# First layer of a graph network: the row gathers in fours with a wait for their landing, in place of waits for VectorE's marks

## Chip, cores and metric

One core of a Trainium2 chip runs one launch of the kernel. The metric is the time of the launch on the device in microseconds (us), lower is better. TensorE, VectorE, ScalarE, GpSimd (POOL in the profile) and SyncE (SP) each have an instruction stream of their own and meet through semaphores.

## The reference

Four graph layers run one after the other on 3,125 nodes of 64 features and 100,000 edges sorted by destination. Only the first concerns this change:

```python
Qh = (x @ Wq.T + bq).reshape(n, H, D)          # H = 4 heads of D = 16
Kh = (x @ Wk.T + bk).reshape(n, H, D)
Vh = (x @ Wv.T + bv).reshape(n, H, D)
Ee = (edge_attr @ We.T + be).reshape(-1, H, D)
score = (Kh[src] * Qh[dst] * (1.0 / np.sqrt(D)) * Ee).sum(-1)
score = jnp.exp(jnp.clip(score, -5.0, 5.0))
msg = Vh[src] * score[..., None]
wV = jax.ops.segment_sum(msg, dst, num_segments=n)
x = _layernorm(x + wV.reshape(n, H * D))
```

The other three layers (a LightGCN, a graph attention, and an attention on edge features) follow, each with a layernorm.

## The kernel before

**Stages.** After a start in which the K and V rows of all nodes are computed and stored in HBM as the table `kv_tab` (one row of 128 floats a node), the first layer goes over the edges in G = 98 groups of 1,024 edges, 8 edges (C = 8) on each of 128 partitions. In the same loop the kernel counts edges between pairs of node tiles (`key_hot`, `lo_hot`, `count`) for the later layers. Then come the layernorm, preparations, and layers two to four; none of those is touched.

**A group on each engine.** SP loads the group's 1,024 source numbers (`idx`) and its edge attributes (`ea`, 256 KB). POOL issues 8 indirect DMAs (line 634), one for each column c, each of which gathers 128 rows of `kv_tab` into `kv[:, s, c, :]`; `kv` and `ea` have RS = 4 slots s, so that a group's rows can be gathered while up to three older groups are unread. VectorE multiplies the K rows with the edge products (line 704) and the queries (line 712), sums over heads (714), clips (716), adds four blocks of counts (698), builds the next group's one-hot matrix (676) and, with ScalarE's exponential, the message (725), then the next group's eight `key_hot` (683), and last adds TensorE's 64-node window of sums to `acc` (736). TensorE counts (837), transposes (795, 803), sums the messages (852) and makes the next group's products (812 to 820).

**What sets the order around the change.** VectorE's line 736 waits for `sum_ok`, which TensorE raises with its last matmul of line 852, and itself raises `slot_free`, on which SP waits before it loads `idx` and `ea` for the group four further on. POOL waits for `idx_in[s]`, so it can never gather into a slot whose reader isn't done. Beside that it waits for `half_done`, a count that starts at 3 and that VectorE raises twice a group, with line 712 and after line 725. By these numbers the second four gathers of a group wait for line 712 of the group before, and the next group's first four follow them at once. VectorE waits for `kv_in[s]` to reach 128 (8 gathers by 16) before line 704. `pass_on` adds 1 to a counter nobody waits for; it turns a wait against a register into one instruction of the engine's queue.

In the rows `shared` is the buffer in which `kv` and `ea` lie, so "shared<-kv_tab,idx" is one gather.

Of the kernel before, what the change touches and what calls it, by code (L numbers as in the profile page):

```python
# [8 lines left out]
ALU, ACT, AX = mybir.AluOpType, mybir.ActivationFunctionType, mybir.AxisListType  # L9
# [7 lines left out]
C = 8  # L17
ST = P * C
G = -(-E // ST)
# [46 lines left out]
def build(nc, x, src, dst, edge_attr_2, edge_attr_64, Wq, bq, Wk, bk, We, be, Wv, bv,  # L66
          attn_w, W_fc, W_attn, W_edge, W_e2n, W_m1, W_m2, out):
    ctx = ExitStack()
    with ctx:
# [9 lines left out]
        def short_sem(name):  # L79


            return nc.alloc_semaphore(name=name)
# [92 lines left out]
        bank = [ctx.enter_context(nc.psum_tensor(f"bank{i}", [P, 512], fp32)) for i in range(8)]  # L175
# [351 lines left out]
        def pass_on(eng):  # L527

            eng.sem_inc(passed, 1)
# [27 lines left out]
        prod = sb("prod", [P, C * D])  # L557
# [21 lines left out]
        def uses(s):  # L579
# [8 lines left out]
        cleared, q_in = short_sem("a_cleared"), short_sem("a_queries")  # L588
        key_ok, lo_ok, count_ok, bank_free = short_sem("a_key"), short_sem("a_lo"), short_sem("a_count"), short_sem("a_count_added")
        count_clear = short_sem("a_count_cleared")  # L590

        half_done = short_sem("a_half_done")
        loop_sems = [begun, slot_free, *idx_in, *ea_in, hot_ok, ea_t, ea_ts, hot_t, hot_ts, ee_ok, qd_ok, sc_ok, ex_ok, msg_ok, sum_ok,
                     cleared, q_in, key_ok, lo_ok, count_ok, bank_free, count_clear, half_done]
        nc.clear_and_free_semaphores(early_sems)
        with nc.Block() as block:
            @block.sync
# [21 lines left out]
            @block.gpsimd  # L619
            def _(pool):  # L620
                nj = sweeps(pool, 1)
                with pool.Fori(0, nj) as j:
                    def gather(g, s, m):

                        pool.wait_ge(half_done, (j * G + g) * 2 + 1)
                        pass_on(pool)
                        pool.wait_ge(idx_in[s], (j * uses(s) + m) * 16)
                        pass_on(pool)
                        for c in range(C):
                            if c == C // 2:  # L630

                                pool.wait_ge(half_done, (j * G + g) * 2 + 2)
                                pass_on(pool)
                            nc.gpsimd.indirect_dma_start(  # L634
                                kv[:, s, c, :], None, kv_tab, bass.IndirectOffsetOnAxis(ap=idx[:, s, c:c + 1], axis=0)
                            ).then_inc(kv_in[s], 16)

                    each(pool, gather)
                    forget_rows(pool, kv_in, slot_free, cleared, (j + 1) * G + RS)

            @block.vector
            def _(dve):
                nj = sweeps(dve, 1)

                dve.sem_inc(slot_free, RS)
                dve.sem_inc(half_done, 3)
                dve.sem_inc(cleared, 1)
                nc.vector.memset(count_i[:, 0:NT * 2 * D], 0)
                nc.vector.memset(msg[:, :, D:D + 1], 1.0)
                nc.vector.memset(qwin[:, :, :, :], 0.0)  # L650
                nc.vector.memset(ones_b[:, :], 1.0)
                rest = be_row[:, :]
                for k in range(BF):
                    nc.vector.tensor_copy(be_part[:, k, :], rest)
                    dve.drain()
                    if k + 1 < BF:
                        nc.vector.tensor_tensor(be_rest[:, k, :], rest, be_part[:, k, :], ALU.subtract)
                        dve.drain()
                        rest = be_rest[:, k, :]
                nc.vector.tensor_scalar(be_rest[:, 0, :], be_part[:, 0, :], ident[0:BF, 0:1], None, ALU.mult)  # L660
                dve.drain()
                for k in range(1, BF):
                    nc.vector.scalar_tensor_tensor(be_rest[:, k % 2, :], be_part[:, k, :], ident[0:BF, k:k + 1], be_rest[:, (k - 1) % 2, :], ALU.mult, ALU.add)
                    dve.drain()
                nc.vector.tensor_copy(be_parts[:, :, :], bc(be_rest[:, (BF - 1) % 2, :], 1, C))
                reset_windows(dve, True)
                dve.sem_inc(bank_free, 2)
                dve.wait_ge(count_clear, 1)
                with dve.Fori(0, nj) as j:
                    dve.wait_ge(cleared, j + 1)  # L670
                    pass_on(dve)
                    start_sweep(dve, begun, True)

                    def node_hots(g, s, m):

                        nc.vector.tensor_tensor(hots[:, s % 2, :, :], bc(dst_rel[:, bass.ds(g, 1), :].rearrange("p g c -> p (g c)"), 2, W),
                                                bc(iota[:, 0:W], 1, C), ALU.is_equal).then_inc(hot_ok, 1)

                    def key_hots(g, s, m):

                        keys = tile_key[:, bass.ds(g, 1), :].rearrange("p g c -> p (g c)")
                        for c in range(C):
                            last = nc.vector.tensor_scalar(key_hot[:, c, :], iota_key[:, :], keys[:, c:c + 1], None, ALU.is_equal)  # L683
                        last.then_inc(key_ok, 1)

                    def front(g, s, m):
                        node_hots(g, s, m)
                        key_hots(g, s, m)

                    def step(g, s, m, after):  # L690

                        n = j * G + g + 1

                        def add_counts(q):

                            at = count[:, :, bass.ds(group_at[q], WC)]
                            dve.wait_ge(count_ok, j * (G * GG) + g * GG + q + 1)
                            nc.vector.tensor_tensor(at, at, bank[6 + q % 2][:, 0:KC].rearrange("p (h w) -> p h w", w=WC),  # L698
                                                    ALU.add).then_inc(bank_free, 1)

                        kvs = kv[:, s, :, :]
                        dve.wait_ge(kv_in[s], m * (16 * C))
                        dve.wait_ge(ee_ok, n)
                        nc.vector.tensor_tensor(prod[:, :].rearrange("p (c f) -> p c f", c=C),
                                                bank[3][:, :].rearrange("p (c f) -> p c f", c=C), kvs[:, :, 0:D], ALU.mult)
                        b, *group_at = nc.values_load_multi_w_load_instructions(
                            base_i[0:1, bass.ds(g, 1), 0:1 + GG].rearrange("a g k -> a (g k)"), engines=[mybir.EngineType.DVE],
                            min_val=0, max_val=NP,
                            skip_runtime_bounds_check_because="start_sweep keeps them within 0 and NP")[1]
                        dve.drain()  # L710
                        dve.wait_ge(qd_ok, n)
                        nc.vector.tensor_tensor(prod[:, :], prod[:, :], bank[4][:, :], ALU.mult).then_inc(half_done, 1)  # L712
                        dve.drain()
                        nc.vector.tensor_reduce(score[:, :], prod[:, :].rearrange("p (a d) -> p a d", d=DH), AX.X, ALU.add)
                        dve.drain()
                        nc.vector.tensor_scalar(score[:, :], score[:, :], -5.0, 5.0, ALU.max, ALU.min).then_inc(sc_ok, 1)  # L716

                        add_counts(0)
                        if after:

                            node_hots(*after)
                        dve.drain()
                        add_counts(1)
                        dve.wait_ge(ex_ok, n)
                        nc.vector.tensor_tensor(msg[:, :, 0:D].rearrange("p c (h d) -> p c h d", h=H),  # L725
                                                kvs[:, :, D:2 * D].rearrange("p c (h d) -> p c h d", h=H),
                                                bc(expo[:, :].rearrange("p (c h) -> p c h", h=H), 3, DH), ALU.mult).then_inc(msg_ok, 1)
                        dve.sem_inc(half_done, 1)
                        for q in range(2, GG):
                            dve.drain()  # L730
                            add_counts(q)
                        if after:

                            key_hots(*after)
                        dve.wait_ge(sum_ok, n)
                        nc.vector.tensor_tensor(acc[0:D + 1, bass.ds(b, W)], acc[0:D + 1, bass.ds(b, W)], bank[5][0:D + 1, 0:W], ALU.add).then_inc(slot_free, 1)  # L736
                        dve.drain()

                    pipelined(dve, front, step)
# [2227 lines left out]
```

## Time and profile before

| what | value |
|---|---|
| time of three runs, median | 2739.47 us (2739.45 to 2748.15) |
| the profiled execution, first to last instruction | 2724.4 us |
| what lies around that span in a run (median less span) | 15.1 us |
| gathers of the first layer, number and busy time | 784, 771.9 us |
| first gather of the layer starts | 51.05 us |
| last step on VectorE (line 736) of the layer | 1466.13 us |
| busy share of the span: TensorE, VectorE, ScalarE, POOL | 55%, 50%, 38%, 47% |

The profiled execution has no run time of its own beside its span, so the span and the 15.1 us around it stand for it. Times in rows are microseconds from the span's start. A gather's row on POOL is the time in which POOL makes its descriptors; the data moves after that. The starts of rows of TensorE are taken from the trace, their ends are modelled. Over half the span, 51 to 1466 us, is the loop that the change touches.

### The profile page before, as it was taken

The numbers are of one execution on the slowest core, as the hardware profiler recorded it, in microseconds if no ns is written. First come the engines' busy times: TensorE is split into PE (matmuls) and PEld (weight loads), VectorE is DVE, ScalarE is ACT, GpSimd is POOL, SyncE is SP. The second block draws the span as 40 slices with busy tenths as digits, with TensorE's granted clock in tenths as the row PEclk, the third lists the DMA queues.
The fourth block names the chain that finished last, engine by engine and source line by source line (L and its number), as shares of the span: only waits on it lengthen the run. The fifth ranks groups of instructions, "written<-read, shape, count | busy, mean of one in ns | idle before, by whom it ended". The sixth has DMA issues, their size and how long they took to land. (4 is left out here: it accounts for less than half of the span.)

```text
span 2724.4 us, 45155 instructions
## 1 busy us (share of the span) xinstructions
PE 1507.1 (55%) x13291; PEld 1250.8 (46%) x13291; DVE 1361.2 (50%) x3516; ACT 1033.2 (38%) x2313; POOL 1291.1 (47%) x1384
## 2 busy tenths in 40 slices
PE   3555555555555555555554875851155555555596
PEld 2444434443444444434443864750144444444585
DVE  6555555555555555555556878851123333333354
ACT  3333333333333333333333905821134444444473
POOL 2555555555555555555552902637444444444400
PEclk7777777777777777777776987965566666666787
DMA  5222222222222222222221200041111111111100
GB/s 116 53 56 58 58 58 57 56 58 58 56 58 58 57 56 59 58 57 55 59 56 52 61 21 1 19 106 34 19 32 32 33 32 32 33 32 32 32 10 14
DMA packets 126436, 128.43 MB, mean 47 GB/s; under 512 B 81780, under 2 KB 89128, under 8 KB 126045
## 3 DMA queue, kind: packets, MB, share of 16 engines
q0 software_dynamic: 37824, 64.91, 10.3%
q1 hardware_dynamic: 62934, 54.96, 7.5%
q10 hardware_dynamic: 25542, 6.81, 1.1%
q8 instruction: 80, 1.31, 0.2%
q14 instruction: 56, 0.45, 0.1%
HBM read 116.63 MB, written 9.93 MB: 46 GB/s over the span
## 5 line engine op out<-in xcount | busy, mean ns | idle before, releaser
L634 POOL DMA_INDIRECT shared<-kv_tab,idx x784 | 771.9, 985 | 679.5 <-DVE prod L712 425.6
L837 PE MATMUL bank<-key_hot,lo_hot 128*128 128x350 f16 x784 | 219.7, 392 | 629.9 <-issue 428.6
L2265 POOL DMA_INDIRECT count<-att_tab,count x302 | 290.9, 963 | 332.0 <-PE bank L2797 209.6
L837 PEld LDWEIGHTS bank<-key_hot,lo_hot 128*128 128x128 f16 x784 | 57.8, 101 | 734.5 <-issue 722.4
L2621 ACT ACTIVATE shared<-shared 128x128 f32<-128x128 bf16 x384 | 162.9, 483 | 322.4 <-remote 221.3
L736 DVE TENSOR_TENSOR acc<-acc,bank 65x64 f32 x98 | 21.3, 217 | 502.7 <-remote 502.0
L780 ACT ACTIVATE expo<-score 128x32 f32<-128x32 f32 x98 | 22.4, 229 | 606.9 <-DVE score L716 606.9
L698 DVE TENSOR_TENSOR count<-count,bank 128x350 f32 x392 | 205.3, 524 | 83.4 <-issue 73.6
L770 ACT ACTIVATE lo_dist<-iota_neg,tile_lo 128x128 f16<-128x128 f32 x784 | 238.5, 389 | 0.0
L2735 PE MATMUL bank<-shared,ad_row 128*128 128x25 bf16 x1152 | 66.9, 178 | 252.5 <-issue 241.6
L2477 DVE TENSOR_TENSOR count<-count,bank 128x500 f32 x96 | 63.6, 662 | 266.8 <-remote 261.5
L683 DVE TENSOR_SCALAR key_hot<-iota_key,tile_key 128x350 f16<-128x350 f16 x784 | 196.1, 321 | 0.0
L852 PEld LDWEIGHTS bank<-hots,msg 128*65 128x65 f32 x1568 | 185.6, 222 | 0.4 <-DVE msg L725 0.4
L852 PE MATMUL bank<-hots,msg 128*65 128x64 f32 x1568 | 181.7, 304 | 0.0
L2735 PEld LDWEIGHTS bank<-shared,ad_row 128*128 128x128 bf16 x1152 | 49.8, 100 | 268.9 <-issue 267.9
L2766 PE MATMUL bank<-shared 128*128 128x150 f32 x768 | 131.9, 313 | 37.2 <-issue 37.2
L812 PE MATMUL bank<-webd,eaT 128*128 128x128 f32 x784 | 142.6, 339 | 0.6 <-issue 0.6
L2806 PE MATMUL bank<-count,tab 128*66 128x88 f32 x1200 | 137.8, 296 | 0.0
L2766 PEld LDWEIGHTS bank<-shared 128*128 128x128 f32 x768 | 111.4, 200 | 50.7 <-issue 39.9
L2806 PEld LDWEIGHTS bank<-count,tab 128*66 128x66 f32 x1200 | 133.7, 186 | 0.9
L2265 POOL DMA_INDIRECT g_edge<-att_tab,count x96 | 90.8, 946 | 86.0 <-PE bank L2797 57.9
L812 PEld LDWEIGHTS bank<-webd,eaT 128*128 128x128 f32 x784 | 131.0, 252 | 1.0 <-issue 1.0
(523 smaller groups left out, 3194.7 us busy)
## 6 DMA issues: line engine op xcount, KB each, us to landing
shared<-in_edge_attr SPq DMA_DIRECT2D x97, 256.0 KB
shared<-kv_tab,idx POOLq DMA_INDIRECT x784
shared<-lo_tab SPq DMA_DIRECT2D x24, 512.0 KB
count<-att_tab,count POOLq DMA_INDIRECT x302
qwin<-q_tab ACTq DMA_DIRECT2D x196, 16.0 KB
kv_tab<-count SPq DMA_DIRECT2D x1, 1600.0 KB, 10.4
idx<-in_src SPq DMA_DIRECT2D x97, 4.0 KB, 1.6
g_edge<-att_tab,count POOLq DMA_INDIRECT x96
```

The lines of the kernel that those rows point to most:

```text
L634: nc.gpsimd.indirect_dma_start(kv[:, s, c, :], None, kv_tab, bass.IndirectOffsetOnAxis(ap=idx[:, s, c:c + 1], axis=0)).then_inc(kv_in[s], 16)
L683: last = nc.vector.tensor_scalar(key_hot[:, c, :], iota_key[:, :], keys[:, c:c + 1], None, ALU.is_equal)
L698: nc.vector.tensor_tensor(at, at, bank[6 + q % 2][:, 0:KC].rearrange("p (h w) -> p h w", w=WC), ALU.add).then_inc(bank_free, 1)
L770: nc.scalar.activation(lo_dist[:, c, :], iota_neg[:, :], ACT.Abs, bias=los[:, c:c + 1])
L812: nc.tensor.matmul(bank[3][:, q * P:(q + 1) * P], eaT[:, q * P:(q + 1) * P], webd[:, :], start=q == 0, stop=False, skip_group_check=True)
L837: last = nc.tensor.matmul(bank[6 + q % 2][:, 0:KC], lo_hot[:, c, :], key_hot[:, c, :], start=i == 0, stop=i == GT - 1)
L852: last = nc.tensor.matmul(bank[5][0:D + 1, 0:W], msg[:, c, :], hots[:, s % 2, c, :], start=c == 0, stop=c == C - 1)
L2265: nc.gpsimd.indirect_dma_start(ring[s][:, j, 0:D + 2], None, att_tab[1], bass.IndirectOffsetOnAxis(ap=src_i[:, t:t + 1], axis=0)).then_inc ...
L2621: nc.scalar.activation(low_w[:, n % LOW_RING, :], low_dist[:, n % LOW_RING, :], ACT.Relu, bias=p, scale=minus_p).then_inc(low_ok, 1)
L2735: last = nc.tensor.matmul(bank[0][:, t * NT:(t + 1) * NT], lo_turned[:, s, t, :], u_parts[:, k, :], start=k == 0, stop=k == 2)
L2766: nc.tensor.matmul(into[:, 0:NT * QW].rearrange("p (h w) -> p h w", w=QW)[:, :, bass.ds(at[j], TW)], low_w[:, n % LOW_RING, :], keys_w[:, ...
L2806: last = nc.tensor.matmul(sum_of[0:D + 2, 0:UW], tab[:, h, 0:D + 2], blocks[:, i % 2, h, :], start=h == 0, stop=h == NT - 1, skip_group_ch ...
```

## The change

VectorE no longer raises `half_done` (line 712, and the `sem_inc` after line 725), and POOL no longer waits for it. POOL waits for `idx_in[s]`, issues four gathers, waits until `kv_in[s]` has 16 for each gather issued so far in this use of the slot (all data of the four has landed), issues the other four, and waits for those as well before it goes to the next group.

```diff
-        half_done = short_sem("a_half_done")
+        STREAK = 4
...
                     def gather(g, s, m):
 
-                        pool.wait_ge(half_done, (j * G + g) * 2 + 1)
-                        pass_on(pool)
                         pool.wait_ge(idx_in[s], (j * uses(s) + m) * 16)
                         pass_on(pool)
                         for c in range(C):
-                            if c == C // 2:
-
-                                pool.wait_ge(half_done, (j * G + g) * 2 + 2)
-                                pass_on(pool)
                             nc.gpsimd.indirect_dma_start(
                                 kv[:, s, c, :], None, kv_tab, bass.IndirectOffsetOnAxis(ap=idx[:, s, c:c + 1], axis=0)
                             ).then_inc(kv_in[s], 16)
+                            if c % STREAK == STREAK - 1:
+
+                                pool.wait_ge(kv_in[s], m * (16 * C) - 16 * (C - 1 - c))
+                                pass_on(pool)
...
                 dve.sem_inc(slot_free, RS)
-                dve.sem_inc(half_done, 3)
...
-                        nc.vector.tensor_tensor(prod[:, :], prod[:, :], bank[4][:, :], ALU.mult).then_inc(half_done, 1)
+                        nc.vector.tensor_tensor(prod[:, :], prod[:, :], bank[4][:, :], ALU.mult)
...
                                                 bc(expo[:, :].rearrange("p (c h) -> p c h", h=H), 3, DH), ALU.mult).then_inc(msg_ok, 1)
-                        dve.sem_inc(half_done, 1)
```

POOL's queue at the head of the first layer's loop, groups with s = 0 and s = 1, before (`a_half_done`, `a_idx0` and so on are the semaphores `half_done`, `idx_in[0]`; a row shows the waits that stand ahead of it):

```order
L627 ISA [waits a_half_done]
L634 DMA shared<-kv_tab,idx 128x128 [waits a_idx0]
L634 DMA shared<-kv_tab,idx 128x128 x3
L632 REGISTER_ALU
L634 DMA shared<-kv_tab,idx 128x128 [waits a_half_done]
L634 DMA shared<-kv_tab,idx 128x128 x3
L625 ISA
L634 DMA shared<-kv_tab,idx 128x128 [waits a_half_done,a_idx1]
L634 DMA shared<-kv_tab,idx 128x128 x3
```

The same place in the changed kernel:

```order
L628 DMA shared<-kv_tab,idx 128x128 [waits a_idx0]
L628 DMA shared<-kv_tab,idx 128x128 x3
L633 ISA
L628 DMA shared<-kv_tab,idx 128x128 [waits a_kv0]
L628 DMA shared<-kv_tab,idx 128x128 x3
L628 DMA shared<-kv_tab,idx 128x128 [waits a_kv0,a_idx1]
L628 DMA shared<-kv_tab,idx 128x128 x3
L628 DMA shared<-kv_tab,idx 128x128 [waits a_kv1]
L628 DMA shared<-kv_tab,idx 128x128 x3
L625 ISA [waits a_kv1]
```

No gather has moved against another; the two waits for VectorE's mark in each group have gone, and a wait for `kv_in` of the slot just written stands after every fourth gather. On the other engines no instruction with a row of its own has moved.

## Rows read from the trace of the kernel before

**Rows 1.** The page's costliest groups, line 634: count, busy, mean ns, idle before it

```profile
L634 POOL DMA_INDIRECT shared<-kv_tab,idx x784 | 771.9, 985 | 679.5 <-DVE prod L712 425.6
```

**Rows 2.** Windows: length, busy of PE, PEld, DVE, ACT, POOL (instructions), clock, DMA

```profile
86.50:1450.00 1363.50, 745.24 (x4655) 578.14 (x4655) 728.58 (x1806) 465.72 (x1140) 746.21 (x760) 0.74 0.22 57
1450.00:1467.00 17.00, 9.64 (x65) 6.99 (x65) 12.87 (x30) 5.13 (x13) 3.93 (x4) 0.71 0.07 17
```

**Rows 3.** Waits from 84 to 1450 us: total us, times, longest

```profile
DVE acc L736 <- remote: 502.0, 96, 5.4
DVE prod L704 <- issue: 31.0, 95, 0.8
POOL shared L634 <- DVE prod L712: 414.5, 95, 5.0
```

**Rows 4.** Timeline of POOL, 617 to 634 us: start, length, idle before

```profile
620.39 0.94 POOL L634 DMA_INDIRECT shared<-kv_tab,idx  x1 [4.22 <-DVE prod L712]
621.63 1.04 POOL L634 DMA_INDIRECT shared<-kv_tab,idx  x1 [0.31 <-issue]
622.98 1.07 POOL L634 DMA_INDIRECT shared<-kv_tab,idx  x1 [0.30 <-issue]
...
625.60 1.03 POOL L634 DMA_INDIRECT shared<-kv_tab,idx  x1 [0.30 <-issue]
...
629.43 0.94 POOL L634 DMA_INDIRECT shared<-kv_tab,idx  x1 [0.30 <-issue]
```

**Rows 5.** Timeline of VectorE in the same stretch

```profile
617.73 0.22 DVE L736 TENSOR_TENSOR acc<-acc,bank 65x64 f32 x1 [5.23 <-remote]
...
618.91 0.69 DVE L712 TENSOR_TENSOR prod<-prod,bank 128x512 f32<-128x512 f32 x1
...
622.55 0.69 DVE L725 TENSOR_TENSOR msg<-shared,expo 128x512 f32<-128x512 f32 x1
...
624.69 2.01 DVE L683 TENSOR_SCALAR key_hot<-iota_key,tile_key 128x350 f16<-128x350 f16 x8
631.87 0.22 DVE L736 TENSOR_TENSOR acc<-acc,bank 65x64 f32 x1 [5.17 <-remote]
```

**Rows 6.** Timeline of TensorE in the same stretch

```profile
624.17 1.96 PE L852 MATMUL bank<-hots,msg 128*65 128x64 f32 x16
```

**Rows 7.** Timeline of POOL, the layer's last four gathers, first and last

```profile
1452.72 0.94 POOL L634 DMA_INDIRECT shared<-kv_tab,idx  x1 [4.37 <-DVE prod L712]
...
1456.62 0.94 POOL L634 DMA_INDIRECT shared<-kv_tab,idx  x1 [0.30 <-issue]
```

**Rows 8.** Timeline of VectorE, the last two groups

```profile
1458.88 0.21 DVE L736 TENSOR_TENSOR acc<-acc,bank 65x64 f32 x1
1459.33 0.69 DVE L704 TENSOR_TENSOR prod<-bank,shared 128x512 f32<-128x512 f32 x1 [0.24 <-DMA shared<-kv_tab,idx]
...
1466.13 0.22 DVE L736 TENSOR_TENSOR acc<-acc,bank 65x64 f32 x1 [0.62 <-PE bank L852]
```

**Rows 9.** Timeline of TensorE, line 852 of the group before the last

```profile
1456.43 1.50 PE L852 MATMUL bank<-hots,msg 128*65 128x64 f32 x16
```

**Rows 10.** Windows behind the last gather, columns as in rows 2

```profile
1458.60:1458.80 0.20, 0.20 (x3) 0.08 (x1) 0.20 (x2) 0.20 (x2) 0.00 (x0) 1.00 0.08 21
...
1458.90:1459.00 0.10, 0.10 (x1) 0.00 (x0) 0.10 (x2) 0.10 (x2) 0.00 (x0) 1.00 0.00 0
```

**Rows 11.** Timeline of POOL, the layer's first twelve gathers: first, third, last

```profile
51.05 1.14 POOL L634 DMA_INDIRECT shared<-kv_tab,idx  x1 [44.86 <-DMA idx<-in_src]
...
53.75 2.19 POOL L634 DMA_INDIRECT shared<-kv_tab,idx  x1 [0.30 <-issue]
...
67.35 0.94 POOL L634 DMA_INDIRECT shared<-kv_tab,idx  x1 [0.30 <-issue]
```

**Rows 12.** Line 625 on POOL's sequencer: ns min/median/max of one

```profile
L625 POOLq FUSED_REGOPS  x5: 108/108/108, 607.4 to 693.1; - x5
```

More of the change, by code:

```diff
@@ L590, in build @@
         count_clear = short_sem("a_count_cleared")
-        half_done = short_sem("a_half_done")
+        STREAK = 4
         loop_sems = [begun, slot_free, *idx_in, *ea_in, hot_ok, ea_t, ea_ts, hot_t, hot_ts, ee_ok, qd_ok, sc_ok, ex_ok, msg_ok, sum_ok,
-                     cleared, q_in, key_ok, lo_ok, count_ok, bank_free, count_clear, half_done]
+                     cleared, q_in, key_ok, lo_ok, count_ok, bank_free, count_clear]
         nc.clear_and_free_semaphores(early_sems)
```

## The prediction

> **What bounds the kernel now.** I read the groups of the page first, then windows by stage, the waits of the loop, and the timelines of one group. The 784 gathers of line 634 are the costliest group of any engine, 771.9 us busy and 679.5 us idle before them [rows 1]. VectorE is busy 728.58 of 1363.50 us in the loop and POOL 746.21 us [rows 2], so no engine is full: two waits share the rest. VectorE loses 502.0 us ahead of line 736, and POOL 414.5 us ahead of a gather, to line 712 of VectorE [rows 3]. The timeline shows how they make one ring. VectorE's line 712 ends at 618.91 + 0.69 = 619.60; POOL starts at 620.39 and issues eight gathers without a stop, until 629.43 + 0.94 = 630.37 [rows 4, 5]. VectorE has done everything of the group but line 736 by about 626.7, TensorE's sums of line 852 are there at 624.17 + 1.96 = 626.13 [rows 5, 6], and still line 736 starts only at 631.87, which is 1.50 us behind the end of the eighth gather. The next line 712 then lets POOL go again. One step is 631.87 - 617.73 = 14.14 us here.
>
> So TensorE's signal for line 852 reaches VectorE 5.7 us late, and always when POOL has stopped. The last groups confirm it. There only four gathers are issued, 1452.72 to 1457.56, TensorE ends line 852 at 1457.93, and line 736 starts at 1458.88, directly behind VectorE's own work [rows 7, 8, 9]. With no gathers behind it the next step takes 1466.13 - 1458.88 = 7.25 us [rows 8]. I read this as: a long unbroken run of gathers holds back TensorE's signals. It is a reading of timelines; it rests on a coincidence seen in every group, not on an experiment.
>
> What a group costs in the mean: the 1363.50 us of the middle window hold 760 gathers, which is 95 groups [rows 2], so **14.35 us**.
>
> **What the change does to POOL.** POOL is freed of VectorE. The indices of the first four groups are loaded ahead, and four slots keep it up to four groups apart, so its pace is set by its own gathers and the two new waits. The sum for one group:
> - Eight gathers at 746.21 / 760 = 0.982 us [rows 2]: 7.85.
> - Six gaps inside two fours at 0.305 [rows 4]: 1.83.
> - Two landings, counted from the end of the fourth gather. Below, the data of the layer's last gather still moves at 1458.6 to 1458.8 [rows 10], 1.24 us behind the gather's end at 1457.56 at the latest instant of that window. Above, VectorE's line 704, which waits for it, starts at 1459.33 [rows 8], 1.77 us behind; its own start takes about 0.1 of that. So 1.24 to 1.67; I take 1.57, nearer the upper, since that one is an actual release and the other only the traffic: 3.14.
> - Two restarts. A wait of the same form (a register compared, then a gather) costs 620.39 - 619.60 = 0.79 from signal to gather [rows 4, 5]: 1.57 for two.
> - Group boundaries. The second wait and line 625's 108 ns [rows 12] now stand behind the landing with no gather over them: about 0.13 in three boundaries of four. The fourth turns POOL's loop. VectorE's turn of its own loop shows in line 704's 0.8 us of issue time against 31.0 / 95 = 0.33 in the mean [rows 3], so about 0.6 more than in a straight step; I take that for POOL too, as an estimate from another engine: (3 x 0.13 + 0.7) / 4 = 0.27.
>
> Together 7.85 + 1.83 + 3.14 + 1.57 + 0.27 = **14.66 us**, against 14.35. The long stall is gone and two pauses of about 2.4 us have taken its place.
>
> **Who is late next.** VectorE waits for the eighth gather's landing, then has about 8 us of its own work and TensorE's until line 736; it needs line 852's signal once per 14.7 us. The run of gathers after it is four long and ends 5.7 us behind the landing, so the signal can pass in the pause, as in rows 7 to 9. Even if it came only with the next landing it would cost VectorE nothing that POOL waits for. What is removed from VectorE, two raises of a semaphore, lay beside other work: nothing. SP's loads start with line 736, which moves from POOL's idle time into the second four gathers; TensorE needs the attributes four groups later: nothing, and I keep 0.1 us for slower landings in the range.
>
> **The sum.** First gather at 51.05, as before. The first twelve took 67.35 + 0.94 - 51.05 = 17.24 us [rows 11], where 12 x 0.982 + 11 x 0.305 = 15.14 would be regular; VectorE's work at the start of the layer disturbs them, and I keep those 2.1 us. The last landing falls at 51.05 + 2.1 + 98 x 14.66 less the last restart and boundary (1.06), which is 1488.8. VectorE then needs what it needed before, from 1459.23 (0.1 ahead of line 704) to 1466.13, 6.9 us [rows 8]: line 736 at 1495.7, where it was 1466.13. That is +29 us, all later stages shifted. On the span 2724.4 + 29 = 2753.4, and with the 15.1 us around it **2768 us**, 1.1% above the median of 2739.5.
>
> **Rule against row.** Gathers 2, 3 and 5 of the run last 1.04, 1.07 and 1.03 us, the others 0.94 [rows 4]; beside them run lines 676 to 725 and the f16 line 683 of VectorE [rows 5]. The Trainium skill (SBUF — State Buffer, section SBUF: two separate sides) says that a VectorE instruction in a two-port mode locks GpSimd out of its port, so that descriptors can't be written until it ends. The trace agrees in kind, by 0.1 us a gather, where the page speaks of full blocking. VectorE's work moves by about 1.5 us against the fours, and line 683 falls into the first pause; if none met a gather, eight at 0.944 would save 0.3 us a group and the answer would be 14.36, no change. I take the old mean, since lines 676 and 725 still meet the first four.
>
> **Rivals.**
> - No change (14.27 to 14.44 a group): the pauses have no work of VectorE under the gathers, or the landing comes at 1.4. 2731 to 2748 us.
> - Faster: the landing is seen as soon as the traffic ends, 1.24. Two times 0.33 less is 14.0, times 98 is 34 less than before: 2705 to 2730. Against it stands the release in rows 8, 1.77 for everything. It decides once landing and restart are under 2.2 together.
> - Faster by another way: a gather that is waited for costs one fixed time. For that mechanism the rows give 0.94 + 1.57 = 2.51 from issue to landing. The Trainium skill (DMA: Bandwidth & Descriptors, section Anatomy of one DMA) gives about 2.0 us plus the bytes at 436 GB/s, 2.15 us for these 64 KB. By that figure a group would be 0.36 x 2 shorter, 13.94, and the kernel some 2700 us; the trace's release speaks against it.
> - Much slower: four gathers already hold TensorE's signals and the second four begin before they are through, so that VectorE's chain needs two pauses for a group and falls behind POOL. It decides when the chain, about 8 us plus the holds, passes 14.7; held once by 5.7 us it is 13.7, held twice 19. With one group in five held twice: 98 x 0.2 x 4.5 = 88 us more than 2768, up to 2850.
>
> **Chances.** The forecast 0.68 (its own range 2749 to 2795: 0.2 us a group either way), no change 0.14, faster by the traffic's end 0.08, by the fixed time 0.03, much slower 0.07. A measurement of this kernel tells about 0.3%, 8 us, from no change. Slower than that 0.74, within it 0.15 (0.01 of it is the forecast's lower end), faster 0.11. The range 2728 to 2800 leaves out the deeper part of faster, the last rival, and the outer ends of the forecast.
>
> **What the profile after would show.** Gathers in fours, every four followed by 2.3 to 2.7 us of idle time that a DMA ended, two such pauses a group, and a start-to-start of 14.5 to 14.9 us over two fours; no wait of POOL for line 712. Line 736 close behind line 683 or in the first pause, its wait for "remote" gone or short, and in its place 5 to 6 us ahead of line 704, ended by the gathers. Were line 736 still at POOL's stop with a 5 us wait, the reading of the held signals would be wrong in its threshold of more than four. What would make the time wrong is the length of the pause: 0.1 us of it is 20 us in all.

## The result and the profile after

| | before | changed |
|---|---|---|
| median of 19 runs | 2748.92 us (2739.45 to 2782.53) | 2776.21 us (2766.4 to 2792.05) |
| ratio | | 1.0098 [1.0074, 1.0123] |
| profiled span | 2724.4 us | 2774.4 us |
| first layer's loop, first gather to last window | 1415.3 us | 1457.8 us |
| rest of the kernel behind it | 1258.0 us | 1258.4 us |

The changed kernel is slower by 1.0%, where 2768 us against 2739.47 was predicted (1.04%, which the prediction calls 1.1%). One thing must be known before the ratios below: the kernel before runs at two levels, about 2749 us here (the upper level) and about 1961 us in most of the later jobs (the lower level), so every experiment is compared only with the kernel before that ran beside it.

From the page of the changed kernel, its span and the groups of a gather and of VectorE's first product (columns as in [rows 1]):

```profile
span 2774.4 us, 44884 instructions
...
L628 POOL DMA_INDIRECT shared<-kv_tab,idx x784 | 777.6, 992 | 723.7 <-DMA shared<-kv_tab,idx 412.0
...
L701 DVE TENSOR_TENSOR prod<-bank,shared 128x512 f32<-128x512 f32 x98 | 67.8, 692 | 602.6 <-DMA shared<-kv_tab,idx 599.7
```

The first of these group rows gives what a group of eight gathers costs. Busy time plus idle time, less the idle time ahead of the layer's first gather, over 98 groups: (777.6 + 723.7 - 52.0) / 98 = 14.79 us. The same sum over [rows 1, 11] is (771.9 + 679.5 - 44.9) / 98 = 14.35. So 0.44 us a group, 43 us in all, 6 of them in busy time and 37 in idle time. POOL's releaser is now a gather, no longer line 712. I use this sum for every kernel below.

The waits from 84 to 1480 us (total us, times, longest), against [rows 3]:

```profile
DVE prod L701 <- DMA shared<-kv_tab,idx: 587.5, 94, 7.3
...
POOL shared L628 <- DMA shared<-kv_tab,idx: 397.6, 165, 3.1
POOL shared L628 <- issue: 250.4, 589, 3.0
```

The wait of VectorE ahead of its window (line 736 before, 732 now) for "remote" has gone from the list ("remote": the profile finds no instruction that ended close before the signal). In its place stands a wait ahead of line 701, the old 704, of 587.5 / 94 = 6.25 us a group, for the gathers.

POOL's timeline, one group of slot 1, and then the next group of slot 2 (start, length, idle before), against [rows 4]:

```profile
606.33 0.95 POOL L628 DMA_INDIRECT shared<-kv_tab,idx  x1 [2.43 <-DMA shared<-kv_tab,idx]
607.59 0.95 POOL L628 DMA_INDIRECT shared<-kv_tab,idx  x1 [0.30 <-issue]
608.84 1.41 POOL L628 DMA_INDIRECT shared<-kv_tab,idx  x1 [0.30 <-issue]
610.55 1.07 POOL L628 DMA_INDIRECT shared<-kv_tab,idx  x1 [0.31 <-issue]
613.99 0.95 POOL L628 DMA_INDIRECT shared<-kv_tab,idx  x1 [2.37 <-DMA shared<-kv_tab,idx]
...
621.25 0.95 POOL L628 DMA_INDIRECT shared<-kv_tab,idx  x1 [2.56 <-DMA shared<-kv_tab,idx]
624.05 0.95 POOL L628 DMA_INDIRECT shared<-kv_tab,idx  x1 [1.85 <-issue]
```

And VectorE in the same stretch, against [rows 5]:

```profile
605.68 0.69 DVE L701 TENSOR_TENSOR prod<-bank,shared 128x512 f32<-128x512 f32 x1 [6.21 <-DMA shared<-kv_tab,idx]
...
608.75 0.69 DVE L673 TENSOR_TENSOR hots<-dst_rel,iota 128x512 f32<-128x512 f32 x1
...
612.27 1.86 DVE L680 TENSOR_SCALAR key_hot<-iota_key,tile_key 128x350 f16<-128x350 f16 x8
614.04 0.21 DVE L732 TENSOR_TENSOR acc<-acc,bank 65x64 f32 x1
620.39 0.69 DVE L701 TENSOR_TENSOR prod<-bank,shared 128x512 f32<-128x512 f32 x1 [6.14 <-DMA shared<-kv_tab,idx]
```

The reader is to see fours with a pause of about 2.4 us behind each, the window's line 732 directly behind the key matrix of line 680, and VectorE idle for 6.2 us until the eighth gather has landed. At 608.84 a gather lasts 1.41 us in place of 0.94 while line 673 runs; that and the 1.85 us "issue" gap at 624.05 are the parts of a group that were not foreseen.

Last, the windows of before and of changed, loop and rest apart (columns as in [rows 2]); the kernel before:

```profile
51.00:1466.40 1415.40, 769.36 (x4802) 595.93 (x4802) 764.48 (x1888) 486.35 (x1178) 771.91 (x784) 0.74 0.22 57
1466.40:2724.40 1258.00, 718.29 (x8375) 638.85 (x8375) 567.54 (x1565) 531.18 (x1095) 513.75 (x591) 0.72 0.14 33
```

the changed kernel:

```profile
58.00:1516.00 1458.00, 773.16 (x4802) 599.49 (x4802) 743.13 (x1888) 486.47 (x1178) 777.59 (x784) 0.73 0.22 56
1516.00:2774.40 1258.40, 708.65 (x8375) 632.12 (x8375) 568.29 (x1565) 533.00 (x1095) 515.24 (x591) 0.73 0.15 33
```

The loop is 42.5 us longer. The two profiles differ by 50.0 because the first gather starts 7.2 us later in this execution (58.21 against 51.05). That is not the change: executions of one and the same changed kernel start it at 58.21 and at 50.57. The windows ahead of the loop, first of the kernel before and then of the changed one, show where the 7.2 us lie:

```profile
0.00:51.00 51.00, 19.49 (x114) 15.98 (x114) 29.21 (x65) 15.65 (x41) 5.42 (x9) 0.87 0.64 115
0.00:58.00 58.00, 26.70 (x114) 24.29 (x114) 29.22 (x64) 15.50 (x41) 5.43 (x9) 0.72 0.56 100
```

The same 114 instructions of TensorE take 26.70 us in place of 19.49, 7.2 more, at a mean granted clock of 0.72 in place of 0.87; the other engines' busy times are equal.

### The profile page after: what moved, and what is told of

Same layout as the page of the kernel before. It is cut to its first block and busy times, and to the rows that moved or that the text cites. A ratio compares the mean times of both kernels' runs of the same rounds, so it can differ in the third digit from the quotient of the medians.

```text
span 2774.4 us, 44884 instructions
## 1 busy us (share of the span) xinstructions
PE 1508.5 (54%) x13291; PEld 1255.9 (45%) x13291; DVE 1340.6 (48%) x3516; ACT 1035.0 (37%) x2313; POOL 1298.3 (47%) x1384
## 5 line engine op out<-in xcount | busy, mean ns | idle before, releaser
L628 POOL DMA_INDIRECT shared<-kv_tab,idx x784 | 777.6, 992 | 723.7 <-DMA shared<-kv_tab,idx 412.0
L701 DVE TENSOR_TENSOR prod<-bank,shared 128x512 f32<-128x512 f32 x98 | 67.8, 692 | 602.6 <-DMA shared<-kv_tab,idx 599.7
L2731 PE MATMUL bank<-shared,ad_row 128*128 128x25 bf16 x1152 | 60.5, 178 | 240.8 <-issue 233.9
L680 DVE TENSOR_SCALAR key_hot<-iota_key,tile_key 128x350 f16<-128x350 f16 x784 | 183.3, 309 | 0.0
```

The lines of the kernel that those rows point to most:

```text
L628: nc.gpsimd.indirect_dma_start(kv[:, s, c, :], None, kv_tab, bass.IndirectOffsetOnAxis(ap=idx[:, s, c:c + 1], axis=0)).then_inc(kv_in[s], 16)
L2731: last = nc.tensor.matmul(bank[0][:, t * NT:(t + 1) * NT], lo_turned[:, s, t, :], u_parts[:, k, :], start=k == 0, stop=k == 2)
```

## The experiments

Theory A, the prediction's: POOL's own round (8 gathers, 2 landings, 2 restarts, a boundary) sets the pace, and a long run of gathers holds TensorE's signals until it ends. Rivals: something else sets the round (VectorE's chain, held twice), the wait itself costs more than the landing, or the removed marks matter by themselves.

**One wait for eight gathers.**

```diff
-        STREAK = 4
+        STREAK = 8
```

> The changed kernel with one landing wait a group, behind the eighth gather (STREAK = 8). Theory A (POOL's own round sets the pace, and a long run of gathers only delays TensorE's signals until it stops): a round is 8 x 0.99 + 7 x 0.305 + 2.6 = 12.7 us, VectorE's line 732 comes 1.4 us behind the eighth gather and is followed by the next line 701 within 0.4 us; 98 x (12.7 - 14.8) = -205 us against the changed kernel, ratio to the kernel before about 0.935. Theory B (VectorE's chain needs a pause in the middle of a group, because the signals of TensorE that it needs are held from the fifth gather on): VectorE falls behind, the four slots fill, and a group costs 14.2 us or more: ratio 0.99 to 1.02.

Measured: 2252.41 us (2249.98 to 2255.15), before beside it 1961.23, ratio 1.1484 [1.1443, 1.1525]. The expected ratios were worked out for the upper level; what can be compared at this one is a group, 13.27 us, 0.6 more than expected. VectorE:

```profile
604.76 0.20 DVE L732 TENSOR_TENSOR acc<-acc,bank 65x64 f32 x1
609.42 0.69 DVE L701 TENSOR_TENSOR prod<-bank,shared 128x512 f32<-128x512 f32 x1 [4.46 <-DMA shared<-kv_tab,idx]
```

and POOL:

```profile
606.32 0.95 POOL L628 DMA_INDIRECT shared<-kv_tab,idx  x1 [0.30 <-issue]
610.29 0.94 POOL L628 DMA_INDIRECT shared<-kv_tab,idx  x1 [3.03 <-DMA shared<-kv_tab,idx]
```

Two things follow. At this level of the kernel a run of eight gathers does not hold TensorE's signals: line 732 starts 1.6 us before the last gather even begins. And the pause is 2.8 to 3.4 us by slot, 3.1 in the mean, in place of 2.4: the packets of the last two gathers end 1.76 and 1.79 us behind POOL's part of them in the median, those of the first six 1.23 to 1.25 (from the trace's packet times). Line 732 lets SP start the 256 KB load of `ea`, and here that falls beside these two gathers. No run leaves that load out, but the other kernels move it. In the changed kernel its packets lie beside the fifth and sixth gather, and those two end 1.67 and 1.68 us behind POOL's part; in the kernel without waits beside the first and second (1.76 and 1.78); in the kernel before they fall into POOL's stop, and no gather is over 1.23. In the changed kernel the eighth gather, for which POOL waits, is not among the late ones; here it is, and the pause is longer.

**No wait at all: only the marks removed.**

```diff
-        STREAK = 4
+        STREAK = 99
```

> The changed kernel with neither marks nor landing waits: POOL gathers without a stop until the four slots are full. Theory A (long runs hold back TensorE's signals): POOL runs up to 32 gathers in one piece, VectorE's line 732 waits for as long as the run lasts, then POOL waits for slots, so the work of both comes one after the other in part: 13 to 15 us a group, ratio 0.95 to 1.03, with waits of line 732 for TensorE of 5 us and more. Theory C (nothing is held; the marks of the kernel before alone made line 736 late): POOL's own 10.0 us a group, ratio about 0.85.

Measured: 1956.76 us (1949.98 to 1962.34), ratio 0.9972 [0.9953, 0.9991], 10.23 us a group. So removing the marks is worth 0.28%, at the edge of what a measurement of this kernel tells from nothing (10.23 against 10.33 us a group below), and at this level all of the change's cost is in the added waits.

**A wait after every two.**

```diff
-        STREAK = 4
+        STREAK = 2
```

> The changed kernel with a landing wait behind every second gather (STREAK = 2). Theory A (each wait costs a pause of 2.35 us on POOL's path, and POOL's path is all): four pauses in place of two, 14.8 + 2 x (2.35 - 0.305) = 18.9 us a group, ratio 1 + 98 x (18.9 - 14.35) / 2749 = 1.16. Theory B (VectorE's chain sets the pace): unchanged, 1.01.

Measured: 2771.0 us (2768.82 to 2773.71), ratio 1.4122 [1.4072, 1.4173], 18.54 us a group. Two more pauses in place of two gaps add 18.54 - 14.79 = 3.75 us, 1.9 each. The two added pauses are 2.36 us in the mean; less the 0.305 us gap that each replaces they add 4.1, and the page's busy time of the gathers, 741.8 us against 777.6, gives 0.37 back. So a wait costs its own pause, and VectorE's chain takes no part.

**Marks and waits together** (the kernel before, with the waits added).

```diff
                             ).then_inc(kv_in[s], 16)
+                            if c % 4 == 3:
+
+                                pool.wait_ge(kv_in[s], m * (16 * C) - 16 * (C - 1 - c))
+                                pass_on(pool)
```

> The kernel before, its marks kept, with the landing wait of the changed kernel added behind each four gathers. Theory A: line 736 is no longer late (it comes with VectorE's own work), line 712 of the next group follows as soon as the gathers land, and the first mark releases POOL 0.1 + 1.5 us behind the landing where the changed kernel restarts at 0.78; so one pause a group is longer by about 1.6 us: 16.3 us a group, ratio 1.07. If the marks cost nothing beside the landing waits: 14.8 us, ratio 1.01.

Measured: 2423.33 us (2420.28 to 2428.4), ratio 1.2358 [1.2311, 1.2406], 15.02 us a group, well under the 16.3 expected. The expectation added the marks' wait to the pauses. By the time that POOL asks, the mark it asks for is long there, so its wait has no landing in it. What is left is 15.02 - 14.79 = 0.23 us a group: the two pauses are 0.4 us longer together (2.51 and 2.82 us in place of 2.35 and 2.59), and the gathers 0.2 us shorter (760.3 us in all in place of 777.6).

**The two kernels once more, side by side.** What had changed in before itself?

> The kernel before, unchanged, for its trace beside the next run. The four runs ahead of this one had the kernel before at 1961 us where the recorded result had 2749. If the chip sets which of the two it is and this is the quick one: about 1961 us, line 736 directly behind line 683, and POOL's eight gathers held up by nothing, near 10 us a group. If it is the slow one: 2749 us and the 5 us wait of line 736 as in rows 3 and 5.

> The changed kernel, unchanged. Theory A (POOL's round alone sets its pace): 14.6 to 14.8 us a group wherever it runs, since no signal of TensorE is in it. Where the kernel before takes 1961 us that is 98 x (14.7 - 10.1) = 450 us more, ratio about 1.23 (between run8_one_wait's 1.148 and run2's 1.412); where it takes 2749 us, 1.01. If the ratio is 1.01 on the quick chip too, the pauses are not what sets its pace.

Measured: before 1960.43 us in a single run, 10.33 us a group. The changed kernel 2401.38 us in the median of four (2396.82 to 2402.03, and one run of 3023.34 that nothing here explains and that the ratio leaves out), before beside it 1964.71, ratio 1.2218 [1.2148, 1.2288]. VectorE in the kernel before at this level:

```profile
600.94 2.00 DVE L683 TENSOR_SCALAR key_hot<-iota_key,tile_key 128x350 f16<-128x350 f16 x8
602.86 0.20 DVE L736 TENSOR_TENSOR acc<-acc,bank 65x64 f32 x1
604.52 0.69 DVE L704 TENSOR_TENSOR prod<-bank,shared 128x512 f32<-128x512 f32 x1 [1.46 <-DMA shared<-kv_tab,idx]
...
613.13 0.20 DVE L736 TENSOR_TENSOR acc<-acc,bank 65x64 f32 x1
```

The 5.2 us ahead of line 736 of [rows 5] is not there, and a step is 613.13 - 602.86 = 10.27 us. The windows of the kernel before here:

```profile
51.00:1074.00 1023.00, 703.14 (x4821) 545.35 (x4822) 756.92 (x1887) 486.20 (x1178) 767.48 (x784) 0.83 0.31 79
1074.00:1958.60 884.60, 685.00 (x8360) 624.17 (x8357) 566.63 (x1565) 527.23 (x1095) 519.35 (x591) 0.83 0.20 47
```

and of the changed kernel:

```profile
50.50:1508.00 1457.50, 771.12 (x4802) 597.69 (x4802) 742.81 (x1886) 486.36 (x1178) 779.78 (x784) 0.73 0.21 56
1508.00:2398.90 890.90, 692.24 (x8375) 630.13 (x8375) 566.19 (x1566) 527.12 (x1095) 520.38 (x591) 0.82 0.20 47
```

The changed loop takes 1457.5 us at this level and 1458.0 at the other. The old loop takes 1023 and 1415, and the rest of the kernel 885 to 891 and 1258. So the level is not made by this loop alone, since untouched stages move with it too, but the changed loop doesn't feel it.

**A wait that ends earlier**: the third gather's landing in place of the fourth's.

```diff
+        kv_near = short_sem("a_kv_near")
...
-                            ).then_inc(kv_in[s], 16)
+                            ).then_inc(kv_near if c in (2, 6) else kv_in[s], 16)
...
-                                pool.wait_ge(kv_in[s], m * (16 * C) - 16 * (C - 1 - c))
+                                pool.wait_ge(kv_near, (g * C + c + 1) // STREAK * 16 if isinstance(g, int) else g * 32 + 16 * (c + 1) // STREAK)
...
-                        dve.wait_ge(kv_in[s], m * (16 * C))
+                        dve.wait_ge(kv_in[s], m * (16 * (C - 2)))
+                        dve.wait_ge(kv_near, (g + 1) * 32)
```

> The changed kernel, but behind each four POOL waits for the third gather's landing and not for the fourth's (gathers 3 and 7 of a group raise a semaphore of their own, kv_near; VectorE waits for both). Theory A (the pause is landing plus restart, on POOL's path): the third lands 1.57 us behind its own end, which is 0.28 behind the fourth's end, so each pause falls from 2.35 to about 1.1 us and a group from 14.79 to 12.3 us: 244 us less than the changed kernel. That is a ratio of 1.10 where the kernel before takes 1961 us, and 0.92 where it takes 2749 us. Rival (on the slow side TensorE's signals need the long pause): there 14.2 us or more, ratio 1.0.

Measured: 2145.74 us (2142.41 to 2148.82), ratio 1.092 [1.0897, 1.0943], 12.17 us a group. POOL, the first gathers of two fours:

```profile
601.52 1.05 POOL L629 DMA_INDIRECT shared<-kv_tab,idx  x1 [1.07 <-DMA shared<-kv_tab,idx]
...
607.58 0.94 POOL L629 DMA_INDIRECT shared<-kv_tab,idx  x1 [1.19 <-DMA shared<-kv_tab,idx]
```

A pause is shorter by the one gather and gap that now cover it, about 1.25 us, and the group by 14.79 - 12.17 = 2.6.

**The same with runs of eight** (`STREAK = 8`, only the seventh gather raises `kv_near`).

> As near4, with one wait a group, behind the eighth gather for the seventh's landing. Theory A: 8 x 0.98 + 7 x 0.305 + 1.1 + 0.3 = 11.4 us a group, 98 x (11.4 - 10.33) = 105 us above the kernel before where that is at POOL's own pace: ratio 1.05; 1.08 if the landing is 0.6 late again because the load of the edge attributes lies on it, as in run8_one_wait. Where the kernel before takes 2749 us and runs of eight hold TensorE's signals: about 12.5 to 14.5 us, ratio 0.93 to 1.01.

Measured: 2076.51 us (2070.98 to 2081.46), ratio 1.0581 [1.056, 1.0603], 11.45 us a group, where 11.4 was expected.

**VectorE's one-hot matrix moved.** Line 673 stands behind all count additions in place of behind the first, with the aim that POOL writes no gather's descriptors beside it.

```diff
                         add_counts(0)
-                        if after:
-
-                            node_hots(*after)
...
                         if after:
+                            node_hots(*after)
                             key_hots(*after)
```

> The changed kernel with VectorE's line 673 (the next group's one-hot matrix, two operands in SBUF) moved behind the four blocks of counts, where POOL is in its first pause. Theory L (VectorE's instruction locks POOL out of its SBUF port; in the changed kernel's traces the third gather of a group takes 1.41, 1.11, 1.28 and 0.95 us by slot, 1.19 in the mean, where others take 0.945): the third gather falls to about 0.95 us, 0.24 x 98 = 24 us less than the changed kernel, 1% . Rival (the third gather is slow for another cause, or line 722, which now comes earlier, takes the place of 673): within 6 us of the changed kernel. VectorE's own chain gets 2 us longer, which its 6 us of waiting cover.

Measured: 2386.52 us (2384.2 to 2387.55), ratio 1.2148 [1.2127, 1.2168], 14.63 us a group, 15 us under the changed kernel's 2401.38 of the job before, where 24 was expected. POOL, the four gathers of slot 2's group, the third and fourth last:

```profile
609.14 0.94 POOL L628 DMA_INDIRECT shared<-kv_tab,idx  x1 [3.11 <-DMA shared<-kv_tab,idx]
611.94 0.94 POOL L628 DMA_INDIRECT shared<-kv_tab,idx  x1 [1.86 <-issue]
613.18 0.94 POOL L628 DMA_INDIRECT shared<-kv_tab,idx  x1 [0.30 <-issue]
614.43 1.31 POOL L628 DMA_INDIRECT shared<-kv_tab,idx  x1 [0.30 <-issue]
```

and on VectorE line 709 (a product with one operand in a PSUM bank) beside the first of them, the message of line 719 beside the second, and line 673 beside the fourth:

```profile
609.06 0.69 DVE L709 TENSOR_TENSOR prod<-prod,bank 128x512 f32<-128x512 f32 x1
...
612.09 0.68 DVE L719 TENSOR_TENSOR msg<-shared,expo 128x512 f32<-128x512 f32 x1
...
614.23 0.69 DVE L673 TENSOR_TENSOR hots<-dst_rel,iota 128x512 f32<-128x512 f32 x1
```

The long gather follows the instruction. In the changed kernel the third gather lasts 1.19 us in the mean of the slots, here 0.945 everywhere; in slot 2 the instruction now meets the fourth in some groups (the row at 614.43), which in the mean is 1.05 us there, as it was 1.03. So the busy time gained all that was expected: 779.8 us fell to 754.2, 26 us. What went back is idle time, 10 us, and most of it is one pause: the one ahead of slot 2's group is 2.90 us in place of 2.55. Line 673 comes later, the window's step behind it too, and with it the load of `ea`, which now lies beside the seventh and eighth gather; slot 1's eighth ends 1.57 us behind POOL's part in the median, in place of 1.24.

**At the upper level.** Three kernels were run once more, each a single time beside the kernel before.

> run8_one_wait once more, for the case that this chip is one on which the kernel before takes 2749 us. There theory A (a run of eight holds TensorE's signals until it stops) gives line 732 only 1.4 us behind the eighth gather, 4 us or more of waiting ahead of it, and 12.7 to 13.5 us a group, 2600 to 2680 us in all. Theory B (the chain of VectorE then needs more than one run) gives 14.2 us or more. Where the kernel before takes 1961 us: 2252 us as before, and nothing new.

> near4 once more, for the case that this chip is one on which the kernel before takes 2749 us. There theory A gives 12.2 us a group and about 2510 to 2530 us in all, against 2749 and 2776, if TensorE's signals pass in pauses of 1.1 us; the rival (they need more) gives 14.2 us or more and 2750. Where the kernel before takes 1961 us: 2146 us as before, and nothing new.

> no_waits once more, for the case that this chip is one on which the kernel before takes 2749 us. There theory A (a long run of gathers holds TensorE's signals, with or without VectorE's marks) gives waits of line 732 of 5 us and more and 13 to 15 us a group; if the marks alone made line 736 late it gives 10.2 us a group and some 2320 us in all. Where the kernel before takes 1961 us: 1957 us as before, and nothing new.

The first two met the lower level: 2248.57 us beside 1960.82, and 2143.26 beside 1964.55, as before. The third met the upper one: 2752.34 us, before beside it 2748.22, 14.38 us a group. Its waits from 84 to 1480 us:

```profile
DVE acc L732 <- remote: 449.8, 88, 5.9
POOL shared L628 <- DMA idx<-in_src: 423.6, 90, 13.3
```

VectorE in its first groups:

```profile
88.53 0.69 DVE L709 TENSOR_TENSOR prod<-prod,bank 128x512 f32<-128x512 f32 x1 [9.14 <-remote]
...
107.76 0.20 DVE L732 TENSOR_TENSOR acc<-acc,bank 65x64 f32 x1
...
601.86 0.22 DVE L732 TENSOR_TENSOR acc<-acc,bank 65x64 f32 x1 [5.16 <-remote]
```

and POOL's last gather before its first stop and the one after it, then the same at a later stop:

```profile
99.62 0.95 POOL L628 DMA_INDIRECT shared<-kv_tab,idx  x1 [0.31 <-issue]
110.61 0.94 POOL L628 DMA_INDIRECT shared<-kv_tab,idx  x1 [10.04 <-DMA idx<-in_src]
...
599.43 0.95 POOL L628 DMA_INDIRECT shared<-kv_tab,idx  x1 [0.30 <-issue]
604.60 0.94 POOL L628 DMA_INDIRECT shared<-kv_tab,idx  x1 [4.22 <-DMA idx<-in_src]
```

With nothing to stop it, POOL issues the 32 gathers of four slots without a pause, until 100.57. VectorE spends that time in waits of up to 9 us for signals of other engines and reaches line 732 for the first time at 107.76, behind the stop. But the wait of 9.14 us ends at 88.53, with POOL in the middle of its run. After that, POOL waits for the indices of a slot, which line 732 lets SP load, about once a group, and the old picture is back: line 732 starts at 601.86, 1.48 us behind the end of the run's last gather, where [rows 4, 5] show 1.50. So the marks are not what made [rows 5] late; runs of eight do it at this level without them, and the slots' turnover takes the marks' place as what stops POOL. In the kernel before all 96 such waits of line 736 end 1.3 to 1.7 us behind a run's last gather; here 5 of 88 end inside a run.

## Why the prediction was right

**The bound.** Right, and shown: POOL's round sets the changed loop. It is 14.79 us at both levels, moves by its pauses with runs of 2, 4 and 8, and by the cover given to a landing in the two kernels that wait for the gather before the last.

**The terms of a group**, as means over the changed kernel's trace:

| term | predicted | measured |
|---|---|---|
| eight gathers | 7.85 | 7.94 |
| six gaps of 0.305 | 1.83 | 1.83 |
| pause between the fours (landing + restart) | 2.355 | 2.35 |
| pause between groups (the same + boundary) | 2.63 | 2.59 |
| "issue" gap of 1.85 in slot 2's group, one loop pass in three | none | 0.12 |
| sum | 14.66 | 14.83 by terms, 14.79 by the page's row |

The landing, taken from the release in [rows 8] and not from the traffic's end in [rows 10], was right to 0.01 us; with that the rivals "faster" and "no change" fell. The fixed time fell as well: from a gather's start to its landing the trace has 0.945 + 2.35 - 0.785 = 2.51 us. The Trainium skill (DMA: Bandwidth & Descriptors, section Anatomy of one DMA) gives about 2.0 us plus the bytes at 436 GB/s, an estimate of 2.15 us for these 64 KB; the trace doesn't agree. The loop's turn on POOL, estimated from VectorE's, is 2.90 - 2.35 = 0.55 us over a straight pause, against the 0.7 that was put in. Two terms were mis-sized: the gathers, where "I take the old mean" missed that line 673 would meet the third gather of most slots (0.95, 1.41, 1.11 and 1.28 us by slot), and the gap in slot 2. Together they are 0.2 us a group; the boundary gave a little back.

**Rule against row.** The prediction found its trace at odds with full blocking, because gathers were longer by 0.1 us only. That reading was wrong: what counts is how much of VectorE's instruction is left when the gather begins. A stretched gather ends 0.81 us behind the end of the instruction that was under way: 608.75 + 0.69 = 609.44 and 608.84 + 1.41 = 610.25 in the changed kernel, 614.92 and 615.74 in the kernel with line 673 moved, 622.55 + 0.69 = 623.24 and 622.98 + 1.07 = 624.05 in [rows 4, 5]. Through the whole traces it is 0.81 to 0.83 us in nearly every such case, behind lines 673 and 722 and behind the f16 line 680 alike. So it costs a gather what is left of the instruction less 0.13 us: 0.60 left gave 0.47. An instruction that starts behind the gather does not stretch it: the message of 612.09 beside the gather of 611.94, which takes 0.94. Nor does one with an operand in PSUM: line 709, of the same size, is as far into a gather (609.06 against 609.14) as line 673 is in the changed kernel, and the gather takes 0.94 us. The rule of the Trainium skill (SBUF — State Buffer, section SBUF: two separate sides) is that VectorE and GpSimd share one pair of ports as an exclusive lock, which the instruction that starts first keeps to its end; the page counts among them VectorE's instructions with two inputs in SBUF, against a GpSimd operation that reads SBUF. The trace agrees: lines 673 and 722 are f32 with two such inputs, and the gather reads its row numbers there.

**Held signals.** The prediction called this "a reading of timelines", and as a statement on the chip it went too far. At the 2749 us level VectorE's waits fit it in both directions: long ones beside runs of eight and more, with and without marks, none in the loop with fours. At the 1961 us level nothing is held, by runs of eight or by the 784 gathers that the kernel without waits issues without a pause. So a long run is needed for it, but isn't enough. The later layers show the same. POOL issues 398 gathers there (line 2265). The waits of the kernel before from 1466 us on at the upper level, and from 1074 us on at the lower:

```profile
DVE count L2477 <- remote: 261.5, 32, 12.1
...
POOL count L2265 <- PE bank L2797: 209.6, 13, 32.9
```

```profile
POOL count L2265 <- issue: 91.8, 301, 0.3
```

At the upper level POOL goes, after two longer runs, in runs of up to 16 with stops that TensorE ends, and VectorE's line 2477 waits up to 12.1 us beside them; at the lower one the gathers go on without a stop, and no wait for "remote" is left on VectorE. Half of the 32 waits end about 3 us behind a run's last gather, the other half inside a run:

```profile
2158.69 0.67 DVE L2477 TENSOR_TENSOR count<-count,bank 128x500 f32 x1 [8.83 <-remote]
...
2159.41 0.94 POOL L2265 DMA_INDIRECT g_edge<-att_tab,count  x1 [0.30 <-issue]
```

So that a signal is held until POOL stops, as the prediction has it, is not shown; that signals come late beside a run is. What sets the level stays open. One chip showed both in two jobs, and the untouched layers change with it under either kernel (1258 against 885 to 891 us), so neither the chip nor this loop decides it. The rival "held twice" was not seen: line 732 never waits in the fours.

**The time around the span.** This step failed. "The 15.1 us around it" was the median less the span, two numbers of different executions; the changed kernel's profiled execution has a time of its own, 2776.21, with 1.8 us around its span of 2774.4. So the profiled execution of before was one near 2726 us, under all its timed runs, if the same 1.8 lies around it. Its quick start at a granted clock of 0.87 may be 7.2 us of that; why it was shorter still isn't known. The number came out near by cancellation: 2768 is 13.3 too high by this, 7.2 too low by the start and about 13 too low by the group's 0.13 us. Profile to profile the change is +50, of which 43 are the change; the medians say +27. Which of these is nearer to what a group costs at the upper level in a timed run can't be told from one profile of each.

**What the change does, then.** At the upper level it replaces a stall of about 5 us a group by two pauses of 2.4, and pays 1% for the difference and the longer gathers. At the lower level there is no stall to replace, and it costs 22%. The kernels that wait one gather earlier, or once for eight, cost less at the lower level; neither ran at the upper level, so whether waiting for the third gather would there beat the kernel before (12.17 us a group against 14.35, if the group is again POOL's) is open. None of the kernels that were run beat the kernel before by more than the 0.3% of the one without waits.

## What to carry to other kernels

A throttle that waits for its own DMAs costs, each time, the landing plus the restart, here 2.35 us; make it wait for the transfer before the last, and the last one's issue pays half of that. Before replacing a stall by a pause of known length, find out whether the stall is there in every job: this one was 4 us a group in one and nothing in the next. Where POOL sets the pace, look at what VectorE has under way when a gather begins: here one with two inputs in SBUF, or in f16, held it up by what was left of it less 0.13 us, and one with an input in PSUM by nothing. And read the time around a span from a run that has both.

## What the runs showed of the hardware

- The same kernel ran at 2749 us and at 1961 us in different jobs, with every stage behind start-up affected; the granted clock, a mean over its two levels of 1.2 and 2.4 GHz, was 0.74 and 0.72 at the one and 0.83 at the other. A lower mean of the granted clock alone is not what makes signals late: the loop with one wait for eight gathers, at the lower level, has 0.75 and no wait of VectorE for "remote", where the loop of before at the upper level has 0.74 and 502.0 us of them.
- At the upper level VectorE waited up to 9.14 us for a signal while 32 gathers were issued back to back, and up to 12.1 us beside runs of up to 16 in a later layer; half of the 32 waits there ended inside a run.
- An f32 instruction of VectorE with two SBUF operands, under way when a gather began, stretched POOL's part of it from 0.945 to 1.41 us; the gather ended 0.81 us behind it. An instruction of the same size with one operand in PSUM left the gather at 0.94 us.
- Gathers that moved beside the 256 KB load of `ea` had their last packet 1.67 to 1.79 us behind POOL's part, others 1.23 to 1.26, in the three kernels that place it beside two gathers of a group.
- A gap of 1.85 us "issue" stands between the first and second gather of slot 2's group in a third of the loop's passes. It is there without the waits too, in the trace of the kernel without waits at the upper level (607.40, behind the gather of 604.60); its cause wasn't looked into.
